# Experts in two halves: the first eight are listed and gathered while the second eight are still searched

## The reference, cut to what matters

```python
probs = softmax(logits, axis=-1)                 # 6000 tokens, 16 experts
scores, tok_idx = top_k(flat_probs, 375)         # each expert takes its best 375 tokens
h = gelu(einsum('ecd,edh->ech', xf[tok_idx], w1) + b1)
y = (einsum('ech,ehd->ecd', h, w2) + b2) * scores[..., None]
routed = zeros.at[tok_idx].add(y)                # scatter-add of the 16 x 375 rows
shared = gelu(xf @ sw1 + sb1) @ sw2 + sb2        # every token
out = h_residual + routed + shared
```

## Time and profile before

| | before |
|---|---|
| median of 3 runs | 1316.1 us |
| profiled execution: its time, its span | 1312.21 us, 1310.5 us |
| phase three begins | 1002.6 us |
| last decision of the search | 1069.3 us |
| all 16 lists ready (`idx`) | 1108.8 us |
| first gather, first scatter | 1109.7, 1127.07 us |
| last scatter issued | 1302.6 us |
| busy: PE, DVE, ACT, POOL | 90%, 68%, 56%, 31% |

### The profile page before, as it was taken

How to read it: one execution, slowest core, us unless ns; L and a number is a source line. 1 busy time by engine, 2 the same in 40 slices (tenths; PEclk the granted TensorE clock), 3 DMA queues, 4 the chain that set the end, 5 groups by cost and what they waited for, 6 DMA issues and landing times. The chain is left out here.

```text
span 1310.5 us, 23146 instructions
## 1 busy us (share of the span) xinstructions
PE 1181.3 (90%) x7812; PEld 992.7 (76%) x7812; DVE 893.2 (68%) x2614; ACT 733.1 (56%) x1847; POOL 405.4 (31%) x379
## 2 busy tenths in 40 slices
PE   6999999999988999999999999999996998766663
PEld 6999999999966777777777777777764767555553
DVE  5656566656659898898998888988864887222120
ACT  2444534444448888888888888888882342222220
POOL 5000001202003442333344324231111001788885
PEclk9999999999999999999999999999997999878876
DMA  5100000000000000000000000000002110445442
GB/s 141 33 13 23 15 16 21 13 24 13 1 25 13 11 16 27 26 26 27 26 20 15 21 27 26 25 14 12 11 21 56 30 33 20 83 91 91 90 90 22
DMA packets 91799, 42.92 MB, mean 33 GB/s; under 512 B 31066, under 2 KB 88007, under 8 KB 91687
## 3 DMA queue, kind: packets, MB, share of 16 engines
q1 hardware_dynamic: 67207, 33.49, 9.4%
q0 software_dynamic: 23808, 6.69, 4.0%
q10 hardware_dynamic: 672, 1.31, 0.3%
HBM read 28.22 MB, written 9.65 MB: 29 GB/s over the span
## 5 line engine op out<-in xcount | busy, mean ns | idle before, releaser
L492 PE MATMUL bank<-h1hl,W2hl 128*128 128x376 f32 x1536 | 277.1, 336 | 2.9 <-DVE h1hl L648 2.9
L492 PEld LDWEIGHTS bank<-h1hl,W2hl 128*128 128x128 f32 x1536 | 263.4, 189 | 7.4 <-issue 4.3
L228 POOL TENSOR_SCALAR cellmax<-grid,csb 125x375 f32<-125x375 f32 x96 | 121.1, 1272 | 392.9 <-DVE csb L221 336.8
L1095 ACT ACTIVATE P<-P,nmax 125x375 f32<-125x375 f32 (+2 forms) x384 | 189.0, 509 | 2.4 <-DVE nmax L1236 2.2
L592 ACT ACTIVATE h<-bank,b2c 128x375 f32<-128x375 f32 x128 | 73.5, 575 | 207.1 <-PE bank L492 207.1
L1236 DVE CUSTOM_DVE_ANT_0 P<-bank,nbias 125x375 f32<-125x375 f32 (+2 forms) x384 | 139.0, 411 | 12.0 <-PE bank L913 12.0
L1105 ACT COPY PT<-bank 128x500 f32<-128x500 f32 (+1 forms) x256 | 128.5, 556 | 8.6 <-PE bank L926 7.9
L913 PE MATMUL bank<-QK 64*125 64x375 f32 (+2 forms) x768 | 116.2, 406 | 13.0 <-DVE nmax L1236 13.0
L926 PE MATMUL bank<-ident,P 125*128 125x125 f32 x768 | 113.5, 275 | 0.2 <-ACT PT L1105 0.2
L1714 ACT ACTIVATE hE<-bank,EB 128x375 f32<-128x375 f32 x64 | 36.7, 573 | 135.0 <-PE bank L1663 132.3
L1121 ACT ACTIVATE tap<-bank,qkd 128x375 f32<-128x375 f32 x128 | 68.5, 570 | 65.3 <-PE bank L962 65.2
(11 more groups left out here) (218 smaller groups left out, 2264.1 us busy)
## 6 DMA issues: line engine op xcount, KB each, us to landing
X<-in_x_dram SPq DMA_DIRECT2D x31, 375.0 KB
EW<-in_L_ffn_w_dram SPq DMA_DIRECT2D x32, 256.0 KB
token_table<-row SPq DMA_DIRECT2D x16, 210.9 KB
tTall<-tT SPq DMA_DIRECT2D x16, 187.5 KB, 2.5
out_dram<-oS SPq DMA_DIRECT2D x15, 187.5 KB
tTall<-in_L_tok_W_dram ACTq DMA_DIRECT2D x1, 1024.0 KB, 8.9
EB<-in_L_ffn_b_dram SPq DMA_DIRECT2D x16, 62.5 KB
tok<-token_table,ids POOLq DMA_INDIRECT x48
```

Of the source, the lines that this page charges most:

```text
L228: nc.gpsimd.tensor_scalar(cellmax[:, k % 2], grid0[:], csb[:, TT_ + k:TT_ + k + 1], None, ALU.max).then_inc(s_cm, 1)
L492: last = nc.tensor.matmul(bank[4 + m % 2][:, :NE], W2hl[:, a, k, m * 128:(m + 1) * 128], h1hl[:, p, b, k], start=(k == 0 and n == 0), stop ...
L1095: nc.scalar.activation(P[:, 2 * r + q, SEG[i]:SEG[i] + w], P[:, 2 * r + q, SEG[i]:SEG[i] + w], ACT.Exp, bias=nmax[:, 2 * r + q, i:i + 1], ...
```

## The change

Experts are handled in two halves of GE = 8. `probsT` becomes [128, 2, N]: a half has 8 experts on 128 partitions (16 sequences x 8), 375 columns. Search and lists run once for each half, over 375 columns. POOL gathers all 8 experts of the first half (24 DMAs) as soon as their indices exist, while DVE searches the second half. The first four experts' layers are written into the second search's last steps and into the second lists. The later 24 gathers stand behind scatters 4 to 12, three or two in a gap; the first four and the last three scatters have none behind them. Other edits: two units a step in place of three; the shared sum is added by DVE straight from PSUM into `Hall` (ACT's copies and `oS` go); expert bias 2 is added by a matmul with a row of ones (one a tile, 3 an expert) and DVE multiplies by the score straight from PSUM; the loops over experts are unrolled and `ids` copies go; `probsT` is written with two DMAs a sequence; sequence 0's shared second layer (`shared_y`) moves ahead of a wait at the end of phase two; Gelu's table is loaded there too.

```diff
@@ phase two, SP
-                        sp.dma_start(probsT[m // 2 * E:(m // 2 + 1) * E, m % 2 * N:(m % 2 + 1) * N], pTs[:]
-                                     ).then_inc(s_ps, 16)
+                        for half in range(2):
+                            sp.dma_start(probsT[m * GE:(m + 1) * GE, half], pTs[half * GE:(half + 1) * GE]
+                                         ).then_inc(s_ps, 16)
@@ phase two, PE (the same two lines go from (b, h) == (B, 7))
+                        if (b, h) == (B, 3):
+                            shared_y(0, 0)
+                            shared_y(0, 1)
@@ phase two, ACT
+                            if m == B - 1:
+                                nc.scalar.activation(warm2[:], zsb[:, 0:4], ACT.Gelu_apprx_tanh)
@@ phase three
-            STEP_UNITS = [(k + 1) * 45 // STEPS for k in range(STEPS)]
+            FIRST_UNITS = 2
+            STEP_UNITS = ([FIRST_UNITS + 2 * (k + 1) for k in range(STEPS)],
+                          [41 + 2 * (k + 1) for k in range(STEPS)])
+            LIST_UNITS = (33, 39, 41)
+            LATE_GATHERS = dict(zip(range(4, 13), (3, 3, 3, 3, 3, 3, 2, 2, 2)))
@@ POOL
-                for e in range(AHEAD):
-                    gather(e, e)
+                for n in range(NT * GE):
+                    gather(n // NT, n % NT)
                 pool.wait_ge(s_first, 16 * HB)
-                def turn(i):
-                    for r in range(RING):
-                        e = RING * i + r
-                        scatter(e, r)
-                        if exists(e + AHEAD):
-                            gather(e + AHEAD, (r + AHEAD) % RING)
+                pool.wait_ge(s_out, 16 * NB)
+                n = NT * GE
+                for e in range(E):
+                    scatter(e)
+                    for _ in range(LATE_GATHERS.get(e, 0)):
+                        gather(n // NT, n % NT)
+                        n += 1
@@ PE
+                def first_layer(e):
+                    ...
+                    for m in range(DC):
+                        wait(pe, s_ehr, 4 * e + m - 1)
+                        nc.tensor.matmul(H_B[m % 2][:, :N], EW1[:, u, m * 128:(m + 1) * 128], tokT[:, u],
+                                         start=True, stop=True).then_inc(s_eh, 1)
+                def search(half, done):
+                    for k in range(STEPS):
+                        pe.wait_ge(s_n, COUNTS * half + 3 * k + 3)
+                        nc.tensor.matmul(SMALL_B[:, TOT:TOT + 3], same[:], cnt[:, 0:3], start=True,
+                                         stop=True).then_inc(s_tot, 1)
+                        shared_units(done, min(STEP_UNITS[half][k], UNITS))
+                        done = min(STEP_UNITS[half][k], UNITS)
+                        if half and k == STEPS - 3:
+                            transpose_tokens(0)
+                            first_layer(0)
+                        if half and k == STEPS - 2:
+                            transpose_tokens(1)
+                            pe.wait_ge(s_yr, NB)
+                            second_layer(0)
+                        if half and k == STEPS - 1:
+                            first_layer(1)
+                shared_units(0, FIRST_UNITS)
+                search(0, FIRST_UNITS)
+                place_totals(0)
+                shared_units(done, LIST_UNITS[0])
+                transpose_chosen(0)
+                shared_units(LIST_UNITS[0], LIST_UNITS[1])
+                collect(0)
+                transpose_lists(0)
+                make_indices(0)
+                shared_units(LIST_UNITS[1], LIST_UNITS[2])
+                search(1, LIST_UNITS[2])
+                place_totals(1)
+                transpose_tokens(2)
+                second_layer(1)
+                transpose_chosen(1)
+                first_layer(2)
+                transpose_tokens(3)
+                second_layer(2)
+                first_layer(3)
+                collect(1)
+                second_layer(3)
+                transpose_lists(1)
+                make_indices(1)
+                transpose_tokens(4)
+                for e in range(4, E):
+                    expert(e)
@@ DVE, decide(half, n): behind the counts
+                        if half and n == STEPS - 3:
+                            take_tokens(0)
+                        if half and n == STEPS - 2:
+                            take_tokens(1)
+                            weigh(0)
@@ DVE
+                def weigh(e):
+                    wait(dve, s_sc, 16 * NT * (e - 1))
+                    for k in range(NT):
+                        dve.wait_ge(s_ey, 2 * e + min(k, 1) + 1)
+                        nc.vector.tensor_scalar(yE[:, e % 2, k], Y_B[min(k, 1)][:PT_, k * C:(k + 1) * C],
+                                                tok[:, e % RING, k, C + e:C + e + 1], None, ALU.mult).then_inc(s_ys, 1)
+                pass_tiles(0)
+                count(1, tries[:, 0])
+                added = summed(LIST_UNITS[1])
+                add_shared(ready, added)
+                pick(0)
+                for n in range(STEPS):
+                    added = decide(1, n, added)
+                select(1, added, NB)
+                take_tokens(2)
+                weigh(1)
+                split_places(1)
+                hot_a(1)
+                take_tokens(3)
+                hot_b(0, SLOT)
+                weigh(2)
+                pass_tiles(1)
+                pick(1, between=(3,))
+                take_tokens(4)
```

More of the change, by code:

```diff
@@ L25 @@
 ROW = C + E
+GE = E // 2
 TEMP, EPS = 1e-5, 1e-5
@@ L1642, in _, with place_totals @@
[L1642 to L1649 removed]
+                def place_totals(half):
+                    pe.wait_ge(s_sel, SELECTED * half + 2)
+                    nc.tensor.matmul(SMALL_B[:, 2:3], same[:], cnt[:, 1:2], start=True, stop=True)
+                    nc.tensor.matmul(SMALL_B[:, 3:4], before[:], cnt[:, 2:3], start=True, stop=True).then_inc(s_m, 1)
@@ new lines, in transpose_chosen @@
+                def transpose_chosen(half):
+                    pe.wait_ge(s_sel, SELECTED * half + 8)
+                    nc.tensor.matmul(SMALL_B[:, 4:5], before[:], place[:, N - 1:N], start=True,
+                                     stop=True).then_inc(s_m, 1)
+                    pe.wait_ge(s_sel, SELECTED * half + 9)
+                    for j in range(NT):
+                        last = nc.tensor.transpose(CHOSEN_B[:PT_, j * 128:(j + 1) * 128],
+                                                   chosen[:, j * PT_:(j + 1) * PT_], ident[:])
+                    last.then_inc(s_m, 1)
@@ new lines, in collect @@
+                def collect(half):
+                    hotA2 = hotA[:].rearrange("p c a e -> p (c a e)")
+                    pe.wait_ge(s_hot, LISTED * half + HOT)
+                    pe.wait_ge(s_c, 3)
+                    for c in range(NT * B):
+                        last = nc.tensor.matmul(LIST_B[:, 0:SLOT * GE], hotA2[:, c * GE * AW:(c + 1) * GE * AW],
+                                                hotB[:, :, c * GE:(c + 1) * GE], start=(c == 0),
+                                                stop=(c == NT * B - 1))
+                    last.then_inc(s_m, 1)
@@ new lines, in second_layer @@
+                def second_layer(e):
+                    u = e % 2
+                    pe.wait_ge(s_ehr, 4 * e + 4)
+                    for t in range(NT):
+                        y = Y_B[min(t, 1)][:PT_, t * C:(t + 1) * C]
+                        if t < 2:
+                            wait(pe, s_ys, NT * (e - 1) + 1 if t == 0 else NT * e)
+                        for k in range(DC):
+                            nc.tensor.matmul(y, hE[:, u, k, t * PT_:(t + 1) * PT_], EW2[:, u, k], start=(k == 0),
+                                             stop=False)
+                        last = nc.tensor.matmul(y, ones_r[0:1, 0:PT_], EB2[0:1, u], start=False, stop=True)
+                        if t != 1:
+                            last.then_inc(s_ey, 1)
@@ L1717, in _, with count @@
-                turns(act, turn)
+                for e in range(E):
+                    u = e % 2
+                    for m in range(DC):
+                        act.wait_ge(s_eh, 4 * e + m + 1)
+                        nc.scalar.activation(hE[:, u, m], H_B[m % 2][:, :N], ACT.Gelu_apprx_tanh,
+                                             bias=EB1[:, u, m:m + 1]).then_inc(s_ehr, 1)
             @block.vector
             def _(dve):
-                def count():
+                def count(half, bits):
@@ new lines, in pass_tiles @@
+                def pass_tiles(half):
+                    for j in range(NT):
+                        dve.wait_ge(s_end, PASSED * half + j + 1)
+                        if j == 0:
+                            nc.vector.tensor_scalar(passed[:], slots[:], ends[:, 0:1], None,
+                                                    ALU.is_ge).then_inc(s_end, 1)
+                        else:
```

(2 more changed lines are left out.)

515 lines of the change are left out of this document (197 added, 318 removed).

## The result

The changed kernel takes 1307.0 us (median of 4 runs, 1306.23 to 1307.83) against 1315.9 of the kernel before (4 runs, 1315.06 to 1317.29): ratio 0.994, 95% interval 0.9925 to 0.9954. The forecast was 1303.5 with a range of 1298 to 1312.5. Of the 12.6 us forecast, 8.9 came.

The account below looks back on a forecast made before the run. POOL's serial chain was taken as the bound: first scatter at 1122.2, plus 162.0 of scatters and 12.45 to the end, with 1.2 for margins 1297.9 against 1310.5. 12.6 less than 1316.1 gives 1303.5, range 1298 to 1312.5.

Parts of the forecast that it names:

- Step 1: End of phase two: with shared_y moved into PE's wait for row, phase three starts at 1000.0, 2.6 us earlier.
- (a): Chain from phase two's end to the first scatter: first scatter at 1122.2, a gain of 4.9 us.
- (b): Stretch of scatters through the experts without half of its gathers: 162.0 us for 170.98, a gain of 9.0.
- Step 2: First search: steps of 3.0 us on average, low clock on the first two units only, fifteen decisions end at 1047.6.
- step 5: Second search to first scatter: twelve steps of 2.97 us, thirteenth 6.6 with expert 0's first layer, yE at 1121.3.
- slower rival: Low clock from the second search's end on, experts included: up to +26 us, put at 1320; chance 0.06.
- Two gathers in a gap at 10.03: Scatter groups with two gathers between: 6.93 + 3.10 us apart, the landing then just past.
- Margins of the first experts: Whether experts 1 to 3 have rows ready for their scatters: margins 0.6, 0.6 and 4 us; 1.2 us allowed.
- three signs: Wrong if first scatter after 1128, one-hots over 9.1 us beside scatters, or POOL waits for yE in mid-experts.
- shared-port rival: DVE's one-hots and POOL's scatters exclude each other: +1 to +7.7 us, 1304.5 to 1311; chance 0.14.
- The steps did not stay longer: Rival on the search: PE-DVE handshakes add 0.2 to 0.4 us in 28 steps, 1309 to 1314.5; chance 0.13.
- PE's pace: Rival among the experts: PE at low clock needs 12 us each, gaps give back all 9.0, 1312.5; chance 0.10.

Follow-up runs that it names:

- second pair of profiles: Changed kernel and kernel before, each run again without edit: 1307.4 us, ratio 0.9934, and 1315.4 us, ratio 1.0004.
- the memsets: Changed kernel with three memsets of an unused tile on POOL ahead of expert 1's scatter, meant to delay it: 1306.5 us, ratio 0.9931.

## Why the prediction was right

**The frame held.** POOL's end is fixed by the first scatter and the stretch of scatters, and both moved the forecast way. Step 1 of (a) was right: `shared_y` in PE's wait takes 2.78 us, phase three starts 9.31 us after POOL's row (forecast 9.23), and putting it back costs 3 us. The count over 375 columns is 0.525 us (forecast 0.53), the step 2.95 (3.0), the first lists with `idx` 24.9 (25.4, though its own terms add up to 25.3), the 24 gathers take 36.3 us (37.2) under the search, and from the last group to the end are 12.53 us (12.45). The table at nothing was right.

**What the 12.6 lacked, in the profile of after.** Of term (a), 3.2 us of 4.9 came, from the row to the first scatter; 2.5 of these are step 1, and steps 2 to 5, the search and the lists in halves, brought 0.6 us where 2.3 were forecast (in the second pair of profiles they brought nothing: 125.28 us after the start of phase three, against 124.28 before). Of term (b), 4.7 of 9.0 came. That is 7.9 us of 13.9, or of 12.7 with the allowance of 1.2.

- *Step 2 and step 5: the clock.* I put the low clock on the first two units alone. It came back in the second step (5.43 us for 3.0) and under expert 0's first layer, where the forecast had "first layer 3.0" and 6.6 for the step; they took 5.31 and 8.91. In other executions the second step is shorter and a low stretch appears after the first lists. Together the two are 4.7 us in the profile. Only 1.7 of them reached the first scatter, because other terms were too high, which is luck: the first decision came 4.59 us after the start of phase three for 5.6, the stretch over the first lists took 27.49 for 28.5, the twelve steps 34.5 for 35.6. That PE's idling brings the low stretches is shown at the end of phase two, in the first step and ahead of expert 0's first layer: with work put in they go, one by one and together, for 5 to 7 us. The slower rival had the mechanism for all experts from 0 on and priced it up to 26 us; expert 0's first layer and a part of expert 4's were hit.
- *Two gathers in a gap at 10.03.* This step was wrong: I added POOL's own time and held the landing to be over. A group that waits for the landing starts 5.94 us after the third scatter's start, and that one 4.53 after its group's: 10.47 in all, which is more than 10.03. Measured are 10.35, 10.46 and 10.45, and 1.2 us are lost. The same sum says that two gathers are free, and the run with the gathers over ten gaps bears it out.
- *Margins of the first experts, 1.2 us.* They cost 2.7: 12.14 and 11.49 for 10.45. For expert 1, DVE's `chosen` waits 2.66 us for a total that PE has behind expert 1's second layer (below), and `yE` stands behind `chosen`; I had that layer ending at the same time as the flags. For expert 2, the one-hots took 1.14 us more. Expert 4's gap, 0.5 us more, I had not looked at: its first layer is at the low clock (4.71 us) and a scatter waits 0.84.
- *Bias products at nothing.* The six records, put at under 1 us, took 1.23, and they stand ahead of a total between the fourteenth and the fifteenth decision (1.5 us with the wait). What they cost in the end is not settled, since the run without them also had the scatter of 7.03 us.

```profile
1135.38 0.62 DVE L1779 SCALAR_TENSOR_TENSOR chosen<-place,bank,chosen 128x375 f32<-128x375 f32 x1 [2.66 <-PE bank L1563]
```

The medians moved by 8.9 us and the traces account for 6 to 8; the rest is within the scatter of the part ahead of the change (990.77 and 994.65 for the same row of the same kernel).

Of the three signs that the prediction named for being wrong, one came in part: POOL waits for `yE`, though at experts 1, 2 and 4 and hardly behind them. The first scatter, at 1125.7, is not after 1128, and the one-hots beside scatters took 8.96 us, just under 9.1. The frame was right and the time is inside a wide range; about half of (b), and most of (a) beyond step 1, did not come.

**The rivals.** What the shared-port rival foretold was there with +1.1 us, the low end of its +1 to +7.7. The run without bias products shows that more can come: one scatter was 5.1 us longer. The Trainium skill, "SBUF — State Buffer", section "SBUF: two separate sides", says that whichever of a DVE instruction in a two-port mode and a GpSimd instruction starts first holds the pair and the other blocks. The eighty undisturbed one-hots without scatters, and the longer ones with them, agree with it that the two hinder each other. The sizes do not: beside three scatters of 6.1 us in all, DVE lost 1.14 us in the changed kernel, so POOL did not hold DVE off for whole scatters; and in the run without bias products POOL was held up over some thirty one-hots in a row (from 1136.72 to the end of the last at 1142.7), not over one instruction. Why POOL got in between them in one kernel and not in the other stays open. A head start of the first scatter is the suspect, argued and not shown: it was ahead of the row by 0.54 to 0.91 us in the changed kernel and with the memsets, where the two scatters behind it passed inside the row, and 2.2 us late in the one case that was held up; the run made to try it missed its condition. The steps did not stay longer, and PE's pace was not the bound from expert 5 on: gaps with three gathers stayed at 11.52 to 11.56 us in the first profile (one of 11.98 in the second).

## What to carry to other kernels

Where another engine's work or a wait in a chain leaves TensorE idle, its next products may run at the low clock, and then cost up to 1.7 times as much (5.31 us for 3.06). When a step is priced at 2.4 GHz, look at what TensorE does in the microseconds ahead of it, and put shared or even unread work there (here worth 5 to 7 us, against 8.9 for the whole change). Where a transfer's landing must be waited for anyway, spread other issues so that each wait holds as many as fit and none holds more: two gathers were free, the third cost 1.1 us. Work moved off the bounding engine brings only the part that no wait fills: gathers of 37 us went from the stretch of scatters, and it became 4.7 us shorter. And a change of many edits should be taken apart: a third of this one's gain is a move of two calls ahead of a wait.

## What the runs showed of the hardware

- An indirect scatter of 125 rows of POOL, 1.95 to 2.06 us at this place in all other profiles, lasted 7.03 us in the one where the first scatter of its group began 2.2 us into a row of 40 bf16 one-hots on DVE, and ended 1.0 us after they had. Scatters behind one that began 0.9 us ahead of the row passed inside it in 2.06 and 2.04 us, and the row was 1.14 us longer. I had expected each to cost a few tenths.
- In the run with the 7.03 us, one step of the chain was 1.5 us shorter and the whole 3.1 us longer.
- The granted clock falls at different places in executions of one kernel: 27.49 or 29.40 us for the same lists, 5.43 or 4.44 for the same step.
